# PEER's lookup: the pair's number innermost, and in the first two batches a sum of the two halves in PSUM

## The reference

```
scores, pk = jax.lax.top_k(all_scores, TOPK)
indices = jnp.take_along_axis(all_indices, pk, axis=-1)
wd = down_embed[indices]
wu = up_embed[indices]
h = jnp.einsum('bnd,bnhkd->bnhk', x, wd)
h = gelu_new(h)
h = jax.nn.softmax(scores, axis=-1) * h
out = jnp.einsum('bnhk,bnhkd->bnd', h, wu)
```

## Time and profile before

| | |
|---|---|
| median of three runs | 458.35 us (457.16 to 460.22) |
| span of the profiled execution, first to last instruction | 456.4 us |
| TensorE busy | 382.1 us, 84% of the span |
| VectorE busy | 328.2 us, 72% |
| ScalarE busy | 197.9 us, 43% |
| GpSimd busy | 105.9 us, 23% |
| mean granted TensorE clock | 0.892 of 2.4 GHz |

### The profile page before, as it was taken

The page is one execution under the profiler, slowest core; times in us unless marked ns, Lnnn a source line. Parts: engine busy times, 40 slices in busy tenths (PEclk is TensorE's granted clock), DMA queues, the critical chain, the costliest instruction groups (busy, mean ns, idle before and its releaser), DMA issues.

```text
span 456.4 us, 8078 instructions
## 1 busy us (share of the span) xinstructions
PE 382.1 (84%) x2848; PEld 294.8 (65%) x2848; DVE 328.2 (72%) x1255; ACT 197.9 (43%) x399; POOL 105.9 (23%) x221
## 2 busy tenths in 40 slices
PE   8977699934445578895999999989999999999896
PEld 4866674314343456663686778877788886797785
DVE  6986657999999999969899788943545434344533
ACT  2443434731201102622576852357833698527221
POOL 2000021132057310172022381160432610010000
PEclk9989899985575596888598999989999999999999
DMA  7950000040000000000000000000000000000000
GB/s 230 338 219 0 1 1 3 0 162 0 1 1 0 1 1 1 2 0 2 0 2 1 1 3 0 1 1 2 13 1 0 1 1 13 1 0 1 13 0 12
DMA packets 5773, 11.81 MB, mean 26 GB/s; under 512 B 2020, under 2 KB 4325, under 8 KB 5222
## 3 DMA queue, kind: packets, MB, share of 16 engines
q1 hardware_dynamic: 5734, 11.31, 7.0%
HBM read 10.78 MB, written 0.52 MB: 25 GB/s over the span
## 4 chain that ended last, share of the span: by engine, by line
PE 37%; DVE 32%; issue 3%; POOL 3%; ACT 2%; DVEq 0%; ACTq 0%; POOLq 0%
PE ps L1195 35%; DVE mx L1099 6%; DVE Xb L1037 5%; DVE HDb L1054 3%; DVE tix L938 2%; DVE Y L1029 2%; DVE pk L947 1%; PE ps L1438 1%; DVE Xb L1049 1%; DVE Sb L1049 1%; DVE xnb L1159 1%; ACT L564 1%; DVE sb_downT L1019 1%; DVE hot L986 1%; DVE hot L984 1%
## 5 line engine op out<-in xcount | busy, mean ns | idle before, releaser
L1195 PEld LDWEIGHTS ps<-dnb,Sb 128*128 128x128 f32 x448 | 55.1, 196 | 9.6 <-issue 3.9
L1195 PE MATMUL ps<-dnb,Sb 128*128 128x128 f32 x448 | 58.0, 282 | 3.8 <-POOL Sb L433 2.3
L1195 PE MATMUL ps<-Y,Xb 128*128 128x32 f16 x512 | 39.9, 250 | 17.6 <-DVE Xb L1037 11.0
L1195 PEld LDWEIGHTS ps<-Y,Xb 128*128 128x128 f16 x512 | 37.2, 162 | 24.3 <-DVE Xb L1037 17.9
L695 ACT ACTIVATE Sb<-ps 128x256 f32<-128x256 f32 x84 | 31.8, 382 | 37.3 <-PE ps L1195 37.3
L1159 DVE SCALAR_TENSOR_TENSOR xnb<-ps,score,xnb 128x128 f32<-128x128 f32 x56 | 17.0, 346 | 42.1 <-PE ps L1195 42.0
L1195 PE MATMUL ps<-ctxTb,sb_guT 128*128 128x256 f32 x168 | 46.0, 404 | 0.1
L1195 PE MATMUL ps<-Xb,sb_guT 128*128 128x256 f32 x168 | 43.7, 390 | 1.8 <-DVE Sb L1169 1.2
L471 ACT ACTIVATE Sb<-ps 128x256 f32<-128x256 f32 (+2 forms) x54 | 26.2, 493 | 37.2 <-PE ps L1195 21.5
L433 POOL TENSOR_TENSOR Sb<-Sb 128x256 f32<-128x256 f32 x28 | 21.2, 766 | 87.0 <-ACT Sb L695 87.0
L564 ACT ACT_TABLE_LOAD x32 | 41.1, 1283 | 0.6
(11 more groups left out here) (278 smaller groups left out, 704.5 us busy)
## 6 DMA issues: line engine op xcount, KB each, us to landing
sb_guT<-in_guT SPq DMA_DIRECT2D x1, 2688.0 KB
dnb<-in_dn SPq DMA_DIRECT2D x1, 1792.0 KB
simb<-in_w_q SPq DMA_DIRECT2D x1, 1024.0 KB, 5.6
simb<-in_w_qT SPq DMA_DIRECT2D x1, 1024.0 KB, 7.2
Gb<-in_ctx SPq DMA_DIRECT2D x1, 512.0 KB, 3.6
Gb<-in_dft SPq DMA_DIRECT2D x1, 512.0 KB, 4.4
sb_x<-in_x SPq DMA_DIRECT2D x1, 512.0 KB
sb_downT<-in_downT SPq DMA_DIRECT2D x1, 512.0 KB, 8.7
```

Of the source, the lines that this page charges most:

```text
L1195: return pe.matmul(o, l, r, start=start, stop=stop)
```

## The change

The view of the PSUM bank changes from (tile, token, half, e) to (tile, half, e, token), so that the token's number within the chunk is innermost, in all batches. The matmul of a token now writes its 32 values 16 elements (64 bytes) apart, ScalarE's copy, VectorE's add and the multiplication's reading of W run over neighbouring elements.

In the batches of `SUMMED`, 0 and 1, a token has two matmuls with the same weights: 16 columns with the high halves, then 16 with the low halves, which is accumulated onto the first. PSUM then holds the sum, in half a bank. `half` returns at once there, and `weigh` is one multiplication that reads PSUM. The signal that a bank is free is `HD_ready`, the multiplication's, in place of `W_taken`. `emptied(m)` says which signal and count chunk m's bank has.

```diff
+        SUMMED = (0, 1)
+        def emptied(m):
+            early = NC * sum(b < m // NC for b in SUMMED)
+            return ("HD_ready", m + 1) if m // NC in SUMMED else ("W_taken", m + 1 - early)
...
             def half(b, c):
+                if b in SUMMED:
+                    return
...
-                act.activation(W[m % 2][:, :, :].rearrange("p s (t e) -> p s t e", e=EH),
-                               ps[:, TOKEN_BANK(b, c), :].rearrange("p (s t k e) -> p s t k e", s=2, k=2, e=EH)[:, :, :, 1, :],
+                act.activation(W[m % 2], ps[:, TOKEN_BANK(b, c), :].rearrange("p (s k c) -> p s k c", s=2, k=2)[:, :, 1, :],
                                ACT.Copy).then_inc(sem("half_ready"), 1)
...
-                v.wait_ge(sem("half_ready"), m + 1)
...
+                hd = HD.rearrange(at, s=2)[:, :, :, c * TC:c * TC + TC]
+                gb = G[:, :, b * L:b * L + L].rearrange(at, s=2)[:, :, :, c * TC:c * TC + TC]
+                if b in SUMMED:
+                    v.wait_ge(sem("W_psum"), m + 1)
+                    v.tensor_tensor(hd, ps[:, TOKEN_BANK(b, c), 0:256].rearrange("p (s e t) -> p s e t", s=2, e=EH), gb,
+                                    ALU.mult).then_inc(sem("HD_ready"), 1)
+                    return
+                _, taken = emptied(m)
+                v.wait_ge(sem("half_ready"), taken)
+                v.tensor_tensor(w, w, ps[:, TOKEN_BANK(b, c), :].rearrange("p (s k c) -> p s k c", s=2, k=2)[:, :, 0, :],
                                 ALU.add).then_inc(sem("W_taken"), 1)
...
+                v.wait_ge(sem("W_taken"), taken)
+                v.tensor_tensor(hd, w.rearrange("p s (e t) -> p s e t", e=EH), gb, ALU.mult).then_inc(sem("HD_ready"), 1)
...
+                signal, count = emptied(m)
                 if bank == 3:
-                    claim(3, "W_taken", m + 1)
+                    claim(3, signal, count)
                 elif c == 1:
                     pe.wait_ge(sem("G_ready"), 2 * EH)
                 else:
-                    pe.wait_ge(sem("W_taken"), m - 1)
-                w = ps[:, bank, :].rearrange("p (q t a) -> p q t a", q=2, t=TC)
-                for t in range(TC):
-                    i = mm(w[:, :, t, :], X[:, c % 2, :, t], Y[:, :, :, :, c * TC + t].rearrange("p q k e -> p q (k e)"))
+                    pe.wait_ge(sem(signal), count - 2)
+                if b in SUMMED:
+                    w = ps[:, bank, 0:256].rearrange("p (q e t) -> p q e t", q=2, t=TC)
+                    for t in range(TC):
+                        mm(w[:, :, :, t], X[:, c % 2, :, t], Y[:, :, 0, :, c * TC + t], True, False)
+                        i = mm(w[:, :, :, t], X[:, c % 2, :, t], Y[:, :, 1, :, c * TC + t], False, True)
+                else:
+                    w = ps[:, bank, :].rearrange("p (q a t) -> p q a t", q=2, t=TC)
+                    for t in range(TC):
+                        i = mm(w[:, :, :, t], X[:, c % 2, :, t], Y[:, :, :, :, c * TC + t].rearrange("p q k e -> p q (k e)"))
```

More of the change, by code:

```diff
@@ L1045, in weigh @@
                 w = W[m % 2]
-                v.wait_ge(sem("half_ready"), m + 1)
                 if m == 0:
                     v.wait_ge(sem("G_ready"), 2 * EH)
-                v.tensor_tensor(w[:, :, :].rearrange("p s (t e) -> p s t e", e=EH),
-                                w[:, :, :].rearrange("p s (t e) -> p s t e", e=EH),
-                                ps[:, TOKEN_BANK(b, c), :].rearrange("p (s t k e) -> p s t k e", s=2, k=2, e=EH)[:, :, :, 0, :],
-                                ALU.add).then_inc(sem("W_taken"), 1)
[L1053 to L1058, removed]
+                at = "p e (s t) -> p s e t"
+                hd = HD.rearrange(at, s=2)[:, :, :, c * TC:c * TC + TC]
[8 more added lines that the diff above has]
+                v.tensor_tensor(w, w, ps[:, TOKEN_BANK(b, c), :].rearrange("p (s k c) -> p s k c", s=2, k=2)[:, :, 0, :],
+                                ALU.add).then_inc(sem("W_taken"), 1)
+                v.wait_ge(sem("W_taken"), taken)
+                v.tensor_tensor(hd, w.rearrange("p s (e t) -> p s e t", e=EH), gb, ALU.mult).then_inc(sem("HD_ready"), 1)
             def added(y, w, x, signal):
```

## The result

| | before | after |
|---|---|---|
| median | 458.1 us (457.16 to 460.22, 4 runs) | 452.59 us (450.81 to 453.13, 4 runs) |
| ratio | | 0.9862, 95% interval 0.9832 to 0.9893 |
| profiled span | 456.4 us | 451.3 us |
| mean granted clock | 0.892 | 0.913 |

A forecast was written before the change was run, and what follows sets the result against it. VectorE was taken to bound batches 0 and 1, with TensorE close behind in batch 1, and TensorE the later batches. Terms of -0.35, +2.5, +2.7, -1.0 and -0.2 us added 3.7 to 458.35: 462.0 us, range 455 to 471.

The forecast's parts named there:

- The second matmul's price: TensorE's lookup, batches 0 and 1: 70 ns per 16-column pair, whatever its columns; 17.9 us more on TensorE over 16 chunks.
- The rival that columns count: TensorE's lookup: a 16-column pair costs 35 ns, TensorE's share stays 1.13 us a chunk; 450 us in all, chance 0.10.
- The multiplication: VectorE's op per chunk: 0.42 us instead of 0.62, reading PSUM in batches 0 and 1, unit stride in 2 and 3.
- Scattered writes: Rival: matmuls writing PSUM 64 bytes apart go from 70 to 120 ns a pair; about +38 us, 500 in all, chance 0.05.
- The rule quoted beside that rival: Trainium skill's PSUM page: any non-contiguous pattern "slows matmuls significantly"; by it the change would be a clear loss.
- An op taken off VectorE is worth something in batches 0 and 1 alone: Whole kernel: VectorE's savings count only in batches 0 and 1, and only as far as TensorE follows.
- the cap of TensorE's gaps: Batches 2 and 3: VectorE's 1.6 us in batch 2 only fills TensorE's 1.44 us of gaps; -1.0 and -0.2 us.
- Batch 0: First batch's lookup: VectorE sheds 4.8 us but spends 4.4 waiting for matmuls, so the mix starts 0.35 us earlier.
- Batch 1's walk: Batch 1, chunk by chunk on TensorE: no gap from 180.3 us, mix at 199.4 instead of 197.06; +2.5 us.
- The clock: Batch 1: longer chunks between wide blocks leave three more blocks at the low clock level, 0.9 us each; +2.7 us.
- the clock stays high: Rival for batch 1: TensorE has fewer gaps and keeps the high clock; -1.9 us, 456.5 in all, chance 0.22.
- The sum: Whole kernel, all terms: -0.35 + 2.5 + 2.7 - 1.0 - 0.2 = +3.7 us.

The follow-up runs named there:

- the second series: The change unaltered, the sum in batch 0 alone, and the change without its second matmul, on one chip: 450.62, 447.38 and 443.65 us.
- The change's repetition: The changed kernel once more, unaltered, as reference on the chip of three other runs: 450.62 us, ratio 0.9881 to the kernel before.

## Why the prediction was wrong, step by step

- **The second matmul's price**, 70 ns a pair for 16 columns: right (66). The rival that columns count gave nearly the measured time, 450, but its mechanism is out: a chunk takes 2.2 us, not 1.3.
- **The multiplication**, 0.42 us: right, in all batches. **Scattered writes**: free, a chunk of 32 columns takes 78 ns a pair in the old and in the new order. The rule quoted beside that rival does not hold for these matmuls; the measurement decides.
- **"An op taken off VectorE is worth something in batches 0 and 1 alone"** and the cap of TensorE's gaps, 38.00 - 36.56, in batches 2 and 3: the step that failed in kind. Forecast -1.2, measured -5.4 (1.6 to 9.3 less), -5.1 by the means of the stages' profiles. Busy time at a low clock was taken for a bound, and in batch 3 the wait was neither engine's but GpSimd's.
- **Batch 0**, -0.35: it is -1.5. The count of eight chunks at 2.25 us was too long by their overlap (2.07); after the change TensorE waits 1.1 and 0.5 us there, and the stage is 18.2 us, not 19.4.
- **Batch 1's walk**, +2.5: right for the clock that it assumed. The kernel before has five blocks of 256 columns or fillers at the low level in this stage (2.09, 2.04, 1.86, 2.09, 1.94), and so has the sum on the old layout (2.09, 2.06, 1.99, 1.86, 1.91), whose stage is 2.0 us longer, 37.66 against 35.71. Against the layout alone the sum costs 3.8 us there (35.11 - 31.29), and 4.1 in the profiles of the second series (35.95 - 31.87), 3.2 in the kernel's time.
- **The clock**, +2.7: the wrong sign, the second step that failed. Batch 1's stretches have 0.74 and 0.96 after 0.74 and 0.80: TensorE waits less (1.2 us in the stage in place of 6.1), and only two blocks of 256 columns or fillers there take 2.1 us. Beside the sum on the old layout, whose chunks and multiplications take the same, three of the change's blocks are 0.84, 0.79 and 0.84 us shorter (shown above), together 2.5, which is all of 37.66 - 35.11. The change's repetition has 35.95, with two more blocks at the low level for all or part of their time (2.09 and 1.60). So the stage is -0.6 and +0.2 beside the kernel before, walk and clock together; what decides the clock in one execution and not in another is not shown. The rival "the clock stays high" was right on this and still 4 us too slow, since it had the same -1.2 for batches 2 and 3 and -0.35 for batch 0.
- **The sum** of the terms by batch: -0.35, +5.2, -1.0, -0.2 forecast; -1.5, -0.6 to +0.2, -2.3 and -2.8 by the means of the stages' profiles, -6.4 to -7.2 in all, or -5.6 to -7.0 with batch 1 from mix to mix (71.7 before, 71.3 and 72.7 after), beside -6.3 measured.

The best version is the layout without the sum, or with it in batch 0 alone: 447.4 to 449.0 us, 3 us below the change.

## What to carry to other kernels

Before a gain is capped by another engine's gaps, look at the granted clock of that stretch: busy time at the low level is not work that must be done, and one wait less may give back the slow block behind it too. Nor is an engine the bound of a stage because it is busy to its end: look at whether what it does there is waited for. Price the parts of a change apart: here the layout gained in every batch, and the sum took a third of it back in one. A step between the values that an op reads was best put on its operand in PSUM, where it cost nothing here.

## What the runs showed of the hardware that was not expected

- A VectorE multiplication of 128 x 256 f32 that reads one SBUF input eight values apart takes 0.62 us, 0.42 side by side; from PSUM 0.42 either way, and the add takes 0.41 with reads of PSUM 16 values apart.
- GpSimd's 0.72 us product takes 1.75 beside VectorE's f16 placement, and VectorE's multiplication of two SBUF inputs up to 0.93 beside that product. With one input in PSUM it is not held: with the sum in all batches one of them (312.80, 0.42) runs beside such a product (312.71, 0.72), and none of the 32 takes more than 0.426. The Trainium skill's page "SBUF — State Buffer" (Who interferes with whom) says that a VectorE instruction with two SBUF inputs contends with a GpSimd one that reads SBUF, and that the order of issue decides which of them blocks. The rows agree.
- An f16 pair of load and matmul costs 66 ns with 16 columns, at 1.2 and at 2.4 GHz, though the weights are those already loaded.
